# The short chunk's down products as two passes of 120 stacked rows and four rests of 24 rows in four row groups

## What is computed

```python
x = x + attention(layernorm(x))                    # q * scan(sigmoid(a), kv)
h = layernorm(x)                                   # 8 groups of 1024 tokens
dispatch, combine = gating_top2(h @ router_w, C)   # C = 256 slots per group and expert
inp = einsum('GSEC,GSM->EGCM', dispatch, h)        # M = 256
hidden = gelu(inp @ w0) * (inp @ w1)               # H = 1368
y = einsum('EGCH,EHM->EGCM', hidden, wo)           # the down products
out = x + einsum('EGCM,GSEC->GSM', y, combine)
```

## Time and profile before

| what | us |
|---|---|
| median of 3 runs (1642.83 to 1646.39) | 1645.25 |
| the profiled execution | 1658.51 |
| its span, first to last instruction | 1656.8 |
| TensorE busy | 1620.5, 98% |
| VectorE busy | 939.8, 57% |
| ScalarE busy | 762.3, 46% |
| GpSimd busy | 506.1, 31% |

### The profile page before, as it was taken

How to read it: one execution, slowest core, us unless ns; L and a number is a source line. 1 busy time by engine, 2 the same in 40 slices (tenths; PEclk the granted TensorE clock), 3 DMA queues, 4 the chain that set the end, 5 groups by cost and what they waited for, 6 DMA issues and landing times.

```text
span 1656.8 us, 22948 instructions
## 1 busy us (share of the span) xinstructions
PE 1620.5 (98%) x8450; PEld 1396.0 (84%) x8450; DVE 939.8 (57%) x1955; ACT 762.3 (46%) x1389; POOL 506.1 (31%) x433
## 2 busy tenths in 40 slices
PE   7999899799999999999999999999999999999998
PEld 6888788688888888888888888888888888888887
DVE  7999754345644564447544654466445644475453
ACT  5777545234433453336333543345334533453333
POOL 2156566563222222222222222222222222222211
PEclk9999999899999999999999999999999999999999
DMA  7553121025422342225211522243223422351211
GB/s 169 160 160 122 53 80 45 13 41 120 86 38 37 81 93 37 39 43 124 39 36 36 135 38 39 39 109 71 39 39 82 93 36 38 64 109 33 36 13 13
DMA packets 193848, 110.94 MB, mean 67 GB/s; under 512 B 96008, under 2 KB 189640, under 8 KB 193736
## 3 DMA queue, kind: packets, MB, share of 16 engines
q1 hardware_dynamic: 165064, 75.37, 18.1%
q0 software_dynamic: 28672, 34.10, 12.8%
HBM read 60.11 MB, written 34.61 MB: 57 GB/s over the span
## 4 chain that ended last, share of the span: by engine, by line
PE 79%; DVE 6%; issue 4%; ACT 3%; SPq 3%; POOL 2%; DMA 2%; another core or an unknown queue 1%; POOLq 0%; ACTq 0%; DVEq 0%
PE bank L1691 23%; PE bank L1714 21%; PE bank L1730 14%; PE bank L1732 8%; PE bank L1503 7%; DVE y L1440 2%; PE bank L1556 1%; PE bank L1705 1%; SPq L509 1%; ACT hhi L922 1%; DVE hlo L1443 1%; SPq L426 1%; POOL slots L658 1%; POOL out L726 1%
## 5 line engine op out<-in xcount | busy, mean ns | idle before, releaser
L726 POOL DMA_INDIRECT out<-xring,slot_records x128 | 215.4, 1683 | 858.1 <-DVE xring L1410 792.9
L922 ACT ACTIVATE hhi<-y 128x512 fp32r<-128x512 f32 (+1 forms) x349 | 220.8, 633 | 508.7 <-DVE y L1440 427.6
L1730 PE MATMUL bank<-wo,hhi 128*128 128x512 f32 (+1 forms) x1276 | 443.7, 385 | 2.0 <-DVE hlo L1443 1.8
L1440 DVE TENSOR_TENSOR y<-bank,sig 128x512 f32<-128x512 f32 x320 | 220.9, 690 | 334.1 <-PE bank L1714 300.8
L1732 PE MATMUL bank<-wo,hlo 128*128 128x256 f32 x1396 | 382.2, 274 | 0.1
L1443 DVE TENSOR_TENSOR hlo<-y,hhi 128x512 fp32r<-128x512 f32 (+1 forms) x349 | 241.6, 692 | 243.9 <-ACT hhi L922 237.6
L912 ACT ACTIVATE sig<-bank 128x512 f32<-128x512 f32 x320 | 189.6, 593 | 209.2 <-PE bank L1691 181.9
L1730 PEld LDWEIGHTS bank<-wo,hhi 128*128 128x128 f32 (+1 forms) x1276 | 239.1, 187 | 50.5 <-DVE hlo L1443 4.0
L1732 PEld LDWEIGHTS bank<-wo,hlo 128*128 128x128 f32 x1396 | 261.6, 187 | 9.2 <-issue 0.8
L1691 PE MATMUL bank<-xThi,whi 128*128 128x512 f32 (+1 forms) x704 | 217.0, 389 | 7.4 <-issue 3.5
L1691 PE MATMUL bank<-xTlo,whi 128*128 128x512 f32 (+1 forms) x704 | 213.2, 383 | 0.0
(11 more groups left out here) (147 smaller groups left out, 1730.6 us busy)
## 6 DMA issues: line engine op xcount, KB each, us to landing
stage<-in_L_ffn_w_kernel SPq DMA_DIRECT2D x160, 128.0 KB
rows<-rows SPq DMA_DIRECT2D x448, 32.0 KB, 1.9
stage<-in_L_ffn_wo_kernel SPq DMA_DIRECT2D x80, 128.0 KB
xring<-in_L_attn_x SPq DMA_DIRECT2D x16, 512.0 KB
out<-xring SPq DMA_DIRECT2D x16, 512.0 KB
x_rows<-rows SPq DMA_DIRECT2D x16, 512.0 KB
slots<-records,sloti POOLq DMA_INDIRECT x128
rows<-x_rows,slot_records POOLq DMA_INDIRECT x128
```

Source lines behind the costliest of these rows:

```text
L726: pool.indirect_dma_start(out_rows, bass.IndirectOffsetOnAxis(idx, 0), ysb[:, t % 2, j, :], None, compute_op=ALU.add).then_inc(added, 16)
L922: act.activation(h_high(e, t, hc)[0:n, :], hf[0:n, hc % 2, :], ACT.Copy).then_inc(h_hi, 1)
L1440: dve.tensor_tensor(hf[0:n, hc % 2, :], up_value(e, t, hc)[0:n, :], gel[0:n, hc % 2, :], ALU.mult).then_inc(mul_done, 1)
L1730: pe.matmul(lines(yb[j][:, :]), high, lines(wo[0:n, hc, :, :].rearrange("p s c -> p (s c)")), start=hc == 0, stop=end, skip_group_check=True)
```

## The change

The rows of the short chunk are laid out anew. Its 88 rows are 64 (`HF`) and a rest of 24 (`HR`). The high operand gets 120 rows: the high parts of rows 0 to 63, the low parts of rows 0 to 31 in rows 64 to 95 (`LOW`), and the high parts of the rest in rows 96 to 119 (`REST`). The low operand gets the high parts of rows 0 to 63 again, the low parts of rows 32 to 63, and the low parts of the rest. The weights are laid out so that two 256-wide matmuls of 120 rows per block (`down_short`) give all partial products but one: the rest's high rows with its low weights. That one is a 256-wide matmul of 24 rows per block (`down_rest`). In the 29 tiles other than `in_drain` and `final` the four of them follow the eight passes, block j with operands at partition 32 j (`h_rest`, `wo_rest`). In the three others each block has its rest behind its two passes, from partition 96.

For that ScalarE makes four copies of 24x128 into `h_rest` and one of 64x512 into `hlo` ahead of the short chunk's L922; VectorE makes three subtractions of 32, 24 and 32 partitions in place of one L1443. The output weights of chunk 8 are loaded by three transfers in place of one, copied by three copies in place of one, and their low parts take five subtractions in place of one. `fill` and `zero` move into the tile `lead`.

```diff
+    LOW, REST = HF, HF + 32
+    assert REST == (T // P - 1) * 32
...
+        wo_rest = sb("wo_rest", [P, D], F32R)
+        h_rest = sb("h_rest", [P, P], F32R)
...
+        fill = lead[:, 0:2 * FJ * REC].rearrange("p (a j c) -> p a j c", a=2, j=FJ)
+        zero = lead[:, 2 * FJ * REC:2 * FJ * REC + D // P]
...
+            for to, a, m in ((0, 0, HF), (LOW, 0, 32), (REST, HF, HR)) if hc == SHORT else ((0, 0, n),):
+                sync.dma_start(stage[to:to + m, s, UCOL:WCOL],
+                               wo_in[bass.ds(e, 1), at + a:at + a + m, :].rearrange("o h m -> h (o m)")).then_inc(
+                                   w_staged[s], 16)
...
+            loads = [7 if c == SHORT else 3 for c in range(s, HC, STAGES)]
...
+            def high_out_weights(hc):
+                raw_out = stage[:, hc % STAGES, UCOL:WCOL]
+                if hc != SHORT:
+                    return act.activation(wo[:, hc, 0, :], raw_out, ACT.Copy)
+                n = REST + HR
+                act.activation(wo[0:n, hc, 0, :], raw_out[0:n, :], ACT.Copy)
+                act.activation(wo[LOW:REST, hc, 1, :], raw_out[32:HF, :], ACT.Copy)
+                return act.activation(wo[REST:n, hc, 1, :], raw_out[REST:n, :], ACT.Copy)
...
+                high_out_weights(hc).then_inc(w_hi0, 1)
...
@@ -919,6 +935,12 @@
...
+                        if hc == SHORT:
+                            for j in range(FJ):
+                                act.activation(h_rest[32 * j:32 * j + HR, :],
+                                               hf[REST:REST + HR, hc % 2, j * P:(j + 1) * P], ACT.Copy)
+                            act.activation(h_low(e, t, hc)[0:HF, :], hf[0:HF, hc % 2, :], ACT.Copy)
+                            n = REST + HR
                         act.activation(h_high(e, t, hc)[0:n, :], hf[0:n, hc % 2, :], ACT.Copy).then_inc(h_hi, 1)
...
+            def low_out_weights(hc):
+                raw_out, high = stage[:, hc % STAGES, UCOL:WCOL], wo[:, hc, 0, :].bitcast(F32)
+                if hc != SHORT:
+                    return dve.tensor_tensor(wo[:, hc, 1, :], raw_out, high, ALU.subtract)
+                rest = slice(REST, REST + HR)
+                for j in range(FJ):
+                    dve.tensor_tensor(wo_rest[32 * j:32 * j + HR, :], raw_out[rest, :], high[rest, :], ALU.subtract)
+                return dve.tensor_tensor(wo[0:HF, hc, 1, :], raw_out[0:HF, :], high[0:HF, :], ALU.subtract)
...
                         if hc == SHORT:
-                            dve.tensor_tensor(hf[HF:n, hc % 2, :], up_gate(e, t, hc)[HF:n, :], gel[HF:n, hc % 2, :],
-                                              ALU.mult).then_inc(rest_made, 1)
+                            dve.tensor_tensor(hf[REST:REST + HR, hc % 2, :], up_gate(e, t, hc)[HF:n, :],
+                                              gel[HF:n, hc % 2, :], ALU.mult).then_inc(rest_made, 1)
...
                         dve.wait_ge(h_hi, HC * FT * e + c + 1)
-                        dve.tensor_tensor(h_low(e, t, hc)[0:n, :], hf[0:n, hc % 2, :], h_high(e, t, hc)[0:n, :].bitcast(F32),
-                                          ALU.subtract).then_inc(h_lo, 1)
+                        high, low = h_high(e, t, hc), h_low(e, t, hc)
+                        if hc == SHORT:
+                            for to, a, m in ((low[LOW:REST], 32, 32), (low[REST:REST + HR], REST, HR),
+                                             (high[LOW:REST], 0, 32)):
+                                split = dve.tensor_tensor(to, hf[a:a + m, hc % 2, :], high[a:a + m].bitcast(F32),
+                                                          ALU.subtract)
+                            split.then_inc(h_lo, 1)
+                        else:
+                            dve.tensor_tensor(low[0:n, :], hf[0:n, hc % 2, :], high[0:n, :].bitcast(F32),
+                                              ALU.subtract).then_inc(h_lo, 1)
...
+            def down_rest(e, t, j):
+                if in_drain(e, t) or final(e, t):
+                    rest, high = slice(REST, REST + HR), h_high(e, t, SHORT)[REST:REST + HR, j * P:(j + 1) * P]
+                else:
+                    rest, high = slice(32 * j, 32 * j + HR), h_rest[32 * j:32 * j + HR, :]
+                return pe.matmul(lines(y_half(e, t, j)), high, lines(wo_rest[rest, :]), start=False, stop=False,
+                                 skip_group_check=True)
+            def down_short(e, t, j):
+                n = REST + HR
+                for h, part in ((h_high, 0), (h_low, 1)):
+                    last = pe.matmul(lines(y_half(e, t, j)), h(e, t, SHORT)[0:n, j * P:(j + 1) * P],
+                                     lines(wo[0:n, SHORT, part, :]), start=False, stop=False, skip_group_check=True)
+                return last
             def down_block(e, t, hc, j):
+                if hc == SHORT:
+                    down_short(e, t, j)
+                    return down_rest(e, t, j)
                 n = columns(hc)
...
+                if hc == SHORT and not (in_drain(e, t) or final(e, t)):
+                    for j in range(FJ):
+                        down_short(e, t, j)
+                    for j in range(FJ):
+                        last = down_rest(e, t, j)
+                    last.then_inc(down, 1)
+                    return
```

16 lines of the change are left out of this document (4 added, 12 removed).

## The result

The changed kernel takes 1696.24 us (1693.88 to 1699.12, four runs) against 1644.99 (1642.83 to 1646.39) on the same chip: ratio 1.0314 (1.03 to 1.0328), 51.2 us slower. It is slower as forecast, but the range ended at 1680 and the sum was 20.7 us. The profiled execution took 1699.12, its span 1697.4. On a second chip the same kernel gave 1.0273 (1.0256 to 1.029), 44.0 us.

What follows compares the result with a forecast made beforehand. The prediction took TensorE as 98% busy, but the ScalarE and VectorE chain as setting the end of last tiles. Its terms, 13.8 + 2.6 + 1.9 + 0.8 + 1.1 + 0.5 = 20.7 us, gave 1666.0 us, range 1654 to 1680.

Steps and rivals of the forecast that it cites:

- last tiles of experts 0 to 6: Seven tiles where the ScalarE and VectorE chain sets the end, less weight-copy waits that the added work covers: 13.8 us slower.
- final tile: wait and clock: Longer TensorE wait for chunk 9's low half, 2.6 us, plus 1.9 us for a lower clock behind it.
- middle tiles of experts 1 to 7: 21 tiles where the grown chain just passes TensorE's own path: 0.04 us each, 0.8 us in all.
- expert 0's second and third tile: One value bank makes chunk 10's value products wait for chunk 9's delayed multiplication: about 0.5 us slower in each.
- The first tile, the attention part and the weights: Expert 0's first tile 0.1 us slower; extra weight work for chunk 8, in the attention part, 0.5 us.
- the chain's growth: Short chunk's multiplication to its last low half: 1.34 us more on ScalarE plus 1.21 on VectorE, 2.55 in all.
- the upper end: Chains and middle tiles with a small ScalarE copy at 0.31 us: 12.8 us more, 1679 us.
- Rival (b): Clock falls in every last tile, not only the final one: 13 us more, 1679 us; chance 0.05.
- The three "unchanged" tiles: Expert 0's first two tiles and the final one: twelve 256-wide matmuls before and after, so no TensorE change counted.
- TensorE in the other tiles: In 29 tiles, eight passes and four rests replace four pairs of matmuls: 1.38 us, the old cost.
- Rival (a): TensorE empties going to 32-row groups and back, 0.70 us: 14 us more over 21 middle tiles, 1680 us; chance 0.16.
- Rivals (c) and (d): Added ScalarE and VectorE work fully hidden, 4.2 us gained, 1641 us, chance 0.06; or half hidden, 1645 us, chance 0.05.

Runs made afterwards that it cites:

- e5: The changed kernel with every added instruction starting at partition 0, the 64x512 copy left out, subtractions cut by columns; one run, middle step 43.64 us.
- e6: The kernel before with only the added ScalarE and VectorE work in each short chunk, TensorE's order unchanged; ratio 1.0276.
- e12: The changed kernel with the four rests behind all eight passes in expert 0's first two tiles; one run, middle step 44.37 us.
- e11: The changed kernel as it is, run on the second chip; ratio 1.0273 to the kernel before.
- e1: The kernel before with TensorE's new order alone, four rests in four row groups in 29 tiles; ratio 1.0013.
- e7: The kernel before with TensorE's new order alone, all four rests on partitions 0 to 23, one row group; one run, middle step 43.99 us.
- e10: The changed kernel with ScalarE's five added copies behind the copy of the high half, with their own semaphore; ratio 1.0149.
- e4: The changed kernel with the small copies and three subtractions reading from the partitions they write, starts still varying; one run, middle step 44.35 us.
- e2: The changed kernel without ScalarE's four 24x128 copies, TensorE's order unchanged; ratio 1.0108.

## Why the prediction was right or wrong

| term, us | forecast | trace of after less before |
|---|---|---|
| last tiles of experts 0 to 6 | 13.8 | 23.9 |
| final tile: wait and clock | 4.5 | 7.6 |
| middle tiles of experts 1 to 7 | 0.8 | 17.0 |
| expert 0's second and third tile | 1.0 | 4.2 |
| sum from the second landmark on | 20.1 | 52.7 |

The first tile, the attention part and the weights (0.6) lie in the part that varies by 18 us between chips and runs, and no run tells about them.

**The step that failed is the chain's growth: 2.55 forecast, 3.30 measured.** Of the 0.75 missing, 0.47 is ScalarE's (1.34, measured 1.81) and 0.29 VectorE's (1.21, measured 1.50). Both were priced back to back by neighbours that start at partition 0. That price is right for such (e5: 0.205), but the added instructions start at 0, 32, 64 and 96 in turn and lose 0.10 to 0.11 each. I looked for the price of a size and not at what else differed between the rows and the new instructions.

**Why 0.75 became 32 us.** The mechanism stood in the prediction, with the slack: 2.5 us in a middle tile, of which the forecast growth used all, with 0.04 over. Beyond that point each further tenth costs 0.1 in every tile. 0.75 x 21 = 15.8 in the middle tiles (measured 17.0 - 0.8 = 16.2), 0.75 x 7 = 5.3 in the last tiles, 0.75 x 2 in expert 0's and 0.75 in the final one: 23 of the 32. A sum that ends right at an edge is the least certain one, and the upper end (1679, with a small copy at 0.31) did include the copy's true price, 0.32. It left out the same for the subtractions, and the other things below.

**The clock.** I had about 2 us of wait for chunk 10 in a last tile and 3.2 at the end; it is two waits of about 1.3 and 1.5, and 3.94. I gave the clock step to the final tile alone, 1.9; it was 6.3 us at half speed, some 3.1. Two last tiles lost 2.0 each and expert 0's 1.1 (47.58 against 46.46 in e6, without a stretch). Rival (b) had the right mechanism for the last tiles, but it hits none to four of the seven and not all. Together 6.3 more (1.2, 4.0 and 1.1). My row for it was misread as well:
```profile
310.13 1.22 PE L1691 MATMUL bank<-xThi,whi 128*128 128x512 f32 x2 [3.10 <-ACT sig L912]
```
This wait lasted from 307.03 to 310.13, and 0.53 granted from 307 to 311 means half speed for 3.8 of the 4 us: the clock had fallen when the wait had hardly begun. Shorter waits stood before it. So the row doesn't say that one wait of 3.1 us brings the clock down, and that the step came in the final tile as forecast is in part luck.

**The three "unchanged" tiles.** Twelve products before and after, but after with four steps into a 24-row product and out: 2.92 for 1.38. In expert 0's second tile it is 1.2 to 1.5 (47.63 to 46.11 in e6, 46.39 in e12). In the final tile the same four steps stand behind the wait: from the last landmark to the end e11 takes 26.83 and e6, with TensorE's old order and as long a stretch at 1.2 GHz, 25.26, 1.6 less. I had counted instructions and not looked at their order. With these 3 us, the 23 and the 6 of the clock, about all of the 32.6 us between forecast and trace is told; it is the account of one trace.

**TensorE in the other tiles: 1.38 forecast, 1.42 measured.** Right in size by luck. I took four rests at full price and no transition; in truth four rests cost one (8 + 1 times 0.115 = 1.03) and the transition 0.385. Rival (a), that TensorE empties on the way in and out, fits as a mechanism: priced 0.70 on top of serial rests, it is 0.385 with concurrent ones. By the figure of the Trainium skill (TensorE: Matmul & The Clock Gate, Part 3: Packing small matmuls) alone the chunk would take an estimated 1.07, 0.15 of it for the rests; e1 has 1.42, with 0.115 for the rests. The Trainium skill (TensorEngine Tiling (Array Packing), Key Properties) also states that a change of the tiling mode drains the engine; it has no price. The traces agree as far as they go: 0.385 in e1, e7 and e12, and in e1 loads that begin only with their matmuls; that the engine is empty in between no row shows. On the kernel before, the new order costs 0.05 a middle tile (e1: 43.64), about 2 us in all; in after the chain ends later and covers it there.

Rivals (c) and (d) fell: VectorE's three subtractions and ScalarE's five copies were hidden only up to 2.5 us in a middle tile. Faster would have needed TensorE to save something, and it saves nothing: 0.345 (three rests of 0.115) is gained in four row groups and 0.385 lost in reaching them. No version run here beats the kernel before.

## What to carry to other kernels

When work is added to an engine that has slack, find the point at which the slack ends and price the addition from above, for what lies beyond is paid in every iteration. Count how often TensorE changes between 128-row and 32-row work, not how many small matmuls there are, and group them: one change cost more than three 256-column matmuls. And put work that only a later step needs behind what the chain waits for: e10 halved the loss by moving five instructions down by one.

## What the runs showed of the hardware that was not expected

- ScalarE and VectorE: an instruction followed by one whose first partition differs is not overlapped with it. 24x128 copies 0.32 apart against 0.205, 32x512 subtractions 0.70 against 0.605. Whether input and output partitions agree makes no difference (e4). A move of the output's first partition is enough (after's four copies all read from 96; VectorE's L1237: 0.43 against 0.33), and on VectorE one of the input's too (0.30 against 0.20).
- TensorE: a step from 120 or 128 rows to 24 and back costs 0.385 us, with 88 as with 120 rows on the other side, in one row group (e7, e12) as in four (e1); four 24-row matmuls in four row groups take the time of one.
- The granted clock: in last tiles with two waits of about 1.3 and 1.5 us and 1.6 us of products between them it fell to 1.2 GHz in some and not in others of the same run, for 3.4 or 6.8 us, and where it fell in after and e11 it did so within 1 us behind the first wait. Waits of 2.6 and 2.7 us in the final tile (e10, e2) did not lower it; behind one of 2.6 us in expert 0's third tile (e10) it fell, and at those of 3.9 us it did each time, before their end or within 0.5 us behind it.
